# A selective-scan mixer: C's rows spread over the partitions by transfers, two banks for B, and one run of TensorE over the chunks

## The chip, the cores and the metric

The program runs on one core of a Trainium2 chip. The metric is the device time of one execution in microseconds (us); of several runs the median counts. The engines of a core are named TensorE (PE in the profile), VectorE (DVE), ScalarE (ACT), GpSimd (POOL) and SyncE (SP). Each has its own instruction stream in strict order, and they wait for each other by semaphores. A wait stops all that follows it on that engine.

## The reference

The program computes four layers one after the other on x of 2 x 1024 x 128: mixer A, a mixture of experts, mixer B, and the experts again. The change touches mixer A alone. Its reference, cut to what matters:

```
xn = rmsnorm(x)
x_part, z = split(xn @ in_proj_w.T)                  # 256 channels each
u = silu(causal_conv4(x_part) + conv_b)
dt, B, C = split(u @ x_proj_w.T, [8, 24])            # 8, 16 and 16 rows
delta = softplus(dt @ dt_proj_w.T + dt_proj_b)
for t: h = exp(delta_t * A) * h + delta_t * B_t * u_t    # 256 channels x 16 states
       y_t = sum over states of h * C_t
out = ((y + u * D) * silu(z)) @ out_proj_w.T + x
```

## The kernel before, in words

Channels lie on the partitions (two groups f of 128) and time along the rows. The 2048 positions are cut into four chunks g of 512; chunks 0 and 1 are the first sequence, 2 and 3 the second, and `half = g % 2` says whether a state is carried in. In a chunk there are 16 states n, with two steps each, one a channel group: s = 2n + f, 32 steps a chunk.

For one state the work goes over all engines:

- TensorE spreads row n of B over the 128 partitions with a matmul against a selecting matrix (L375, bank B), and row n of C in the same way (L378, bank C). `accumulate(n)` adds hc of both groups to the sums Y by matmuls with the unit matrix (L390); at n = 0 it first puts in u * D (L388, `skip`). An f32 matmul of 128x512 is two records in the trace.
- ScalarE writes the decay exp(delta * A) of a step into one of three banks (L520, three steps ahead of the scan at most), and copies the spread row of C to c_sb (L526), which has two places. In even chunks it saves the last column of h (L511).
- VectorE multiplies delta * u by the row of B for both groups at once (`times_b`, L592) and scans (L607). `times_b(n + 1)` stands between the two scans of state n.
- GpSimd multiplies h by the row of C (L678) into hc, which has four places; so has h.

Beside it the next chunk is prepared, through one PSUM bank O that is used in turn (`in_turn`): two convolutions (TAPS0, TAPS1: eight records each, L319), x_proj (XPROJ, L337), two dt_proj (DT0, DT1, L343), two products for z (Z0, Z1, L325), and for the chunk before, the output projection (PROJECT, L349). Which state each stands behind is written out by hand in the TensorE stream, as are ScalarE's reads of the bank in `between` (steps 3, 5, 12, 17, 19, 25, 27; at 6 the two Silus with their table loads, at 20 and 21 the softplus) and GpSimd's additions and products (steps 21, 23, 25). VectorE multiplies the finished sums of the chunk before by silu(z) after state 1 (`gate`, L574), adds the projection after state 3 (`add`, L579) and makes the low rows after state 6 (`low_rows`, L567: B and C are kept as a rounded high part and a rest, both in `rows`). `accumulate(0)` of a chunk overwrites Y and so waits for the gate.

`half_sequence` of TensorE (L368 to L414) orders a chunk: broadcast(0), TAPS0, broadcast(1), then for n from 2 to 15 broadcast(n), accumulate(n - 2) and the piece of other work that is due, and at the end accumulate(14) and accumulate(15). broadcast(n) waits for times_b(n - 1), since B has one bank.

Before the loop (L416 to L434, L534 to L557, L623 to L653) the norm is made, and chunk 0 is prepared with seven products in banks 0 to 3; ScalarE does the absolute value and the Relu of the softplus (L456, L457) and two copies of z (L555). SyncE issues loads of weights at the start of the stage (L303 to L310) and has nothing to do after them until the next stage.

Of the kernel before, what the change touches and what calls it, by code (L numbers as in the profile page):

```python
# [16 lines left out]
P = 128  # L17
# [56 lines left out]
def cols(c):  # L74
    return slice(c * CH, (c + 1) * CH)
# [169 lines left out]
def mixer_a_stage(k, d):  # L245
# [6 lines left out]
    def sem(name):  # L252
# [4 lines left out]
    DEPTH = 4  # L257
    w_in = sb("w_in", [P, 2 * DI])
# [11 lines left out]
    dt_row = sb("dt_row", [40, T])  # L270
# [3 lines left out]
    c_sb = sb("c_sb", [P, 2, CH])  # L274
    state = sb("state", [P, STEPS])
    yz = sb("yz", [P, FT, CH])
    Y, B, O, C, A = 0, 2, 3, 4, 5
# [3 lines left out]
        o_read, u_ready, rows_high, dt_kept, rows_done, rest_done, exp_done, log_done, delta_ready, du_ready, \  # L281
        z_ready, b_ready, c_ready, c_copied, decay_ready, bu_ready, scanned, saved, hc_ready, y_added, yz_ready, \
        x_folded = [sem(n) for n in (
            "w_loaded taps_loaded pad_zero folded taps_ready skip_ready sel_set a_ready first_ready first_read o_ready "
            "o_read u_ready rows_high dt_kept rows_done rest_done exp_done log_done delta_ready du_ready "
            "z_ready b_ready c_ready c_copied decay_ready bu_ready scanned saved hc_ready y_added yz_ready "
            "x_folded").split()]
# [11 lines left out]
    with stage, nc.Block() as block:  # L299

        @block.sync
        def _(sp):
# [7 lines left out]
            sp.dma_start(k.xn_rows[0:1, :], d["eye"][0:1, :]).then_inc(k.first_row, 16)  # L310

        @block.tensor
        def _(pe):

            def convolution(c, f, bank):
                b, t0 = divmod(c * CH, SEQ)
                for tap in range(TAPS):
                    off = PADC + t0 - (TAPS - 1) + tap
                    last = nc.tensor.matmul(ps[:, bank, :], w_tap[:, f, tap, :], xp[:, b, off:off + CH],  # L319
                                            start=(tap == 0), stop=(tap == TAPS - 1))  # L320
# [20 lines left out]
            def dt_proj(c, f, bank):  # L341
                pe.wait_ge(dt_kept, c + 1)
                return nc.tensor.matmul(ps[:, bank, :], w_dt[32:40, f * P:(f + 1) * P], dt_row[32:40, cols(c)],  # L343
# [8 lines left out]
            def in_turn(g, what):  # L352
# [3 lines left out]
                if what in (TAPS0, TAPS1):  # L356
                    last = convolution(g + 1, what - TAPS0, O)
                elif what == PROJECT:
# [9 lines left out]
            def half_sequence(g):  # L368
                at = cols(g)

                def broadcast(n):
                    m = g * NST + n
                    if m:
                        pe.wait_ge(bu_ready, m)
                    nc.tensor.matmul(ps[:, B, :], sel[:, n, :], rows[:, at], start=True, stop=True).then_inc(b_ready, 1)  # L375
                    if m:
                        pe.wait_ge(c_copied, m)
                    nc.tensor.matmul(ps[:, C, :], sel[:, NST + n, :], rows[:, at], start=True, stop=True)\  # L378
                        .then_inc(c_ready, 1)

                def accumulate(n):
                    for f in range(FT):
                        s = n * FT + f
                        if n == 0:
                            if g:
                                pe.wait_ge(yz_ready, (g - 1) * FT + f + 1)
                            u_done(g)
                            nc.tensor.matmul(ps[:, Y + f, :], skip[:, f, :], u[:, f, at], start=True, stop=False)  # L388
                        pe.wait_ge(hc_ready, g * STEPS + s + 1)
                        nc.tensor.matmul(ps[:, Y + f, :], k.eye[:, :], hc[:, s % DEPTH, :],  # L390
                                         start=False, stop=(n == NST - 1)).then_inc(y_added, 1)

                if g:
                    pe.wait_ge(o_read, use(g - 1, XPROJ) + 1)
                broadcast(0)
                if g + 1 < NCH:
                    in_turn(g, TAPS0)
# [1828 lines left out]
```

## Time and profile before

| | us |
|---|---|
| median of 3 runs | 1179.07 |
| runs | 1178.4 to 1183.63 |
| the profiled execution's own time | 1185.69 |
| its span in the profile | 1183.9 |
| mixer A: loop, first times_b to end of the last scan | 44.90 to 342.3 |
| mean granted TensorE clock of the profiled execution | 0.938 |
| busy over the span: PE, DVE, ACT, POOL | 1032.6, 750.7, 641.3, 575.4 |

The span is shorter than the execution's time by what lies around it. Mixer A's stage ends at about 348.5 us; the rest of the span belongs to the other three layers. In the profile a granted clock of 1.0 is 2.4 GHz and 0.5 is 1.2 GHz; a value between them is a mean over a stretch that has both. PE's busy time is modelled and records overlap a little; PEld are its weight loads. The names with "a_" are mixer A's tiles, "ps" is PSUM.

### The profile page before, as it was taken

To read this page: it belongs to the slowest core of one execution; us is meant where nothing else is said; L and a number is where in the kernel's file an instruction comes from. 1 tells how busy PE (TensorE), PEld (TensorE's weight loads), DVE (VectorE), ACT (ScalarE), POOL (GpSimd) and SP (SyncE) were. 2 spreads that over 40 slices of the span, in tenths; PEclk is the share of its full clock that TensorE was granted. 3 is DMA by queue.
4 is the path that set the end of the run, shared out by engine and by line. 5 is a ranking of instruction groups with operands and counts; after the bars stand their busy time and mean duration, and the time that the engine had idled before them with its cause. 6 is when DMAs were issued, how large, how long until landed. Compare 5 with 4: busy or idle time off the path is not lost. (4 is left out here: it accounts for less than half of the span.)

```text
span 1183.9 us, 16592 instructions
## 1 busy us (share of the span) xinstructions
PE 1032.6 (87%) x4894; PEld 721.0 (61%) x4894; DVE 750.7 (63%) x1163; ACT 641.3 (54%) x1222; POOL 575.4 (49%) x455
## 2 busy tenths in 40 slices
PE   5788787886888789999999887896986899999997
PEld 2222322322227568999999543663664689999996
DVE  4578597677965955555555567764549545555555
ACT  5567464573645344555555386676553345555553
POOL 2268367465650088853671273641000888353732
PEclk9889899887997999999999987997979999999999
DMA  4000000000013022411210300000140214111103
GB/s 132 0 1 0 1 0 0 1 0 1 0 59 113 1 69 70 102 52 52 70 52 15 92 22 1 1 1 0 34 139 0 64 44 126 59 52 54 54 28 112
DMA packets 47906, 49.52 MB, mean 42 GB/s; under 512 B 5000, under 2 KB 39568, under 8 KB 47824
## 3 DMA queue, kind: packets, MB, share of 16 engines
q1 hardware_dynamic: 42832, 38.22, 10.5%
q0 software_dynamic: 4992, 10.23, 3.5%
q8 instruction: 48, 0.79, 0.3%
q14 instruction: 34, 0.28, 0.1%
HBM read 38.08 MB, written 10.36 MB: 41 GB/s over the span
## 5 line engine op out<-in xcount | busy, mean ns | idle before, releaser
L678 POOL TENSOR_TENSOR a_hc<-a_h,a_c_sb 128x512 f32<-128x512 f32 x128 | 160.3, 1268 | 125.5 <-DVE a_h L607 112.0
L390 PE MATMUL ps<-a_hc,eye 128*128 128x512 f32 x256 | 148.0, 684 | 17.2 <-POOL a_hc L678 15.4
L592 DVE TENSOR_TENSOR a_b_u<-a_du,ps 128x1024 f32<-128x1024 f32 x64 | 77.0, 1204 | 58.0 <-PE ps L375 58.0
L390 PEld LDWEIGHTS ps<-a_hc,eye 128*128 128x128 f32 x256 | 44.2, 201 | 91.6 <-POOL a_hc L678 59.9
L520 ACT ACTIVATE ps<-a_delta,a_neg_a 128x512 f32<-128x512 f32 x128 | 86.8, 685 | 20.0 <-DVE a_h L607 19.9
L870 POOL CAST g_ring_rounded<-g_ring 128x1876 fp32r<-128x1876 f32 x8 | 14.1, 1758 | 154.2 <-DVE g_table L1385 104.2
L607 DVE TENSOR_TENSOR_SCAN a_h<-ps,a_state,a_b_u 128x512 f32<-128x512 f32 x64 | 79.1, 1268 | 2.8 <-ACT ps L520 2.5
L607 DVE TENSOR_TENSOR_SCAN a_h<-ps,a_b_u 128x512 f32<-128x512 f32 x64 | 75.3, 1208 | 6.9 <-ACT ps L520 6.7
L526 ACT ACTIVATE a_c_sb<-ps 128x512 f32<-128x512 f32 x64 | 38.0, 593 | 76.6 <-PE ps L378 49.7
L1014 PE MATMUL ps<-g_ring_rounded,g_q_hi_rounded 128*128 x312 | 77.0, 337 | 0.0
L1014 PE MATMUL ps<-f_ring_rounded,f_q_hi_rounded 128*128 x312 | 77.0, 337 | 0.0
L1016 PE MATMUL ps<-f_ring_rounded,f_q_lo_rounded 128*128 x312 | 69.6, 223 | 0.0
L1016 PE MATMUL ps<-g_ring_rounded,g_q_lo_rounded 128*128 x312 | 69.6, 223 | 0.0
L870 POOL CAST f_ring_rounded<-f_ring 128x1876 fp32r<-128x1876 f32 x8 | 14.1, 1760 | 113.4 <-DVE f_table L1385 69.6
L1450 DVE TENSOR_TENSOR g_prods<-g_work,ps 128x470 f32<-128x470 f32 x78 | 49.8, 638 | 28.0 <-PE ps L1042 28.0
L1450 DVE TENSOR_TENSOR f_prods<-f_work,ps 128x470 f32<-128x470 f32 x78 | 49.8, 638 | 27.5 <-PE ps L1042 27.5
L1040 PE MATMUL ps<-f_ring_rounded,f_work_rounded 128*128 x156 | 62.3, 399 | 1.9 <-DVE f_work_rounded L1441 1.5
L1040 PE MATMUL ps<-g_ring_rounded,g_work_rounded 128*128 x156 | 62.4, 400 | 1.7 <-DVE g_work_rounded L1441 1.3
L1155 ACT ACTIVATE g_work<-ps 128x470 f32<-128x470 f32 x78 | 44.0, 563 | 31.3 <-PE ps L1042 31.3
L1155 ACT ACTIVATE f_work<-ps 128x470 f32<-128x470 f32 x78 | 43.9, 563 | 31.2 <-PE ps L1042 31.2
L1014 PEld LDWEIGHTS ps<-g_ring_rounded,g_q_hi_rounded 128*128 128x128 f32 x312 | 58.9, 189 | 2.8
L1014 PEld LDWEIGHTS ps<-f_ring_rounded,f_q_hi_rounded 128*128 128x128 f32 x312 | 58.9, 189 | 2.8
(451 smaller groups left out, 2965.6 us busy)
## 6 DMA issues: line engine op xcount, KB each, us to landing
f_ring<-in_gu SPq DMA_DIRECT2D x16, 469.0 KB, 4.4
g_ring<-in_gu SPq DMA_DIRECT2D x16, 469.0 KB, 4.4
f_ring<-in_dn SPq DMA_DIRECT2D x8, 512.0 KB, 6.1
g_ring<-in_dn SPq DMA_DIRECT2D x8, 512.0 KB, 5.6
xn_rows<-f_work SPq DMA_DIRECT2D x8, 256.0 KB, 2.7
f_rows<-token_rows SPq DMA_DIRECT2D x8, 256.0 KB, 4.8
xn_rows<-g_work SPq DMA_DIRECT2D x8, 256.0 KB, 2.8
g_rows<-token_rows SPq DMA_DIRECT2D x8, 256.0 KB, 4.8
```

What stands on the lines that cost most here:

```text
L390: nc.tensor.matmul(ps[:, Y + f, :], k.eye[:, :], hc[:, s % DEPTH, :], start=False, stop=(n == NST - 1)).then_inc(y_added, 1)
L520: nc.scalar.activation(ps[:, A + m % NA, :], delta[:, f, cols(g)], ACT.Exp, scale=neg_a[:, f, n:n + 1])\
L526: nc.scalar.activation(c_sb[:, n % 2, :], ps[:, C, :], ACT.Copy).then_inc(c_copied, 1)
L592: nc.vector.tensor_tensor(decayed_in[:, p:p + FT, :], du[:, :, cols(g)], ps[:, B, :].unsqueeze(1).to_broadcast([P, FT, CH]), ALU.mult)\
L607: nc.vector.tensor_tensor_scan(h[:, s % DEPTH, :], ps[:, A + m % NA, :], decayed_in[:, s % DEPTH, :], initial, ALU.mult, ALU.add).then_inc ...
L678: nc.gpsimd.tensor_tensor(hc[:, s % DEPTH, :], h[:, s % DEPTH, :], c_sb[:, n % 2, :], ALU.mult)\
L870: nc.gpsimd.tensor_copy(high, raw).then_inc(w_high, 1)
L1014: nc.tensor.matmul(ps[:, Y2, 0:2 * P], q_hi[:, j % 2, a], in_ring(place, w, w + 2 * P), start=(i == 0), stop=False, skip_group_check=True)
L1016: last = nc.tensor.matmul(ps[:, Y2, 0:P], q_lo[:, j % 2, a], in_ring(place, w, w + P), start=False, stop=(i == TILES - 1), skip_group_chec ...
L1040: nc.tensor.matmul(out, xt[:, 0, j % 2, :], w_hi, start=True, stop=False)
L1155: nc.scalar.activation(gates[:, half, 0:HALVES[half]], ps[:, 2 * half, 0:HALVES[half]], ACT.Silu)\
L1450: nc.vector.tensor_tensor(prods[:, j % 2, half * H0:half * H0 + HALVES[half]], gates[:, half, 0:HALVES[half]], ps[:, 2 * half + 1, 0:HALVE ...
```

## The change

Row n of C no longer goes through TensorE, bank C and ScalarE. ScalarE keeps all 40 rows of x_proj's result as they are (x_rows, in place of the 8 rows of dt); SyncE stores C's 16 rows of the chunk in DRAM (c_rows) and then, for each state, issues a transfer that reads one row of 512 values into all 128 partitions of c_sb, which has four places (RING). GpSimd waits for the transfer. The bank that C held goes to B, which alternates between banks 2 and 3; O is bank 4.

TensorE's, VectorE's and ScalarE's streams no longer stop at a chunk's end: broadcast(m) is followed by accumulate(m - 2) for m from 0 to 63, and the first product with B of the next chunk stands between the last two scans. The last three saves of an even chunk come in the first steps of the next. The convolutions are issued in two halves, behind states 0 and 1 (TAPS0) and 2 and 3 (TAPS1); PROJECT, XPROJ, DT0 and DT1 come one state later. ScalarE's reads, the Silus (step 9) and the softplus (steps 21, 22), VectorE's `add` and `low_rows`, and GpSimd's pieces (21, 23, 27) move too. Before the loop VectorE does the two Relus and the two copies of z that ScalarE did.

The diff, cut to its core (runs of removed lines that the listing above shows are left out):

```diff
--- before.py
+++ after.py
@@ -255,6 +255,7 @@
...
     DEPTH = 4
+    RING = 4
     w_in = sb("w_in", [P, 2 * DI])
...
@@ -267,24 +268,26 @@
...
     rows = sb("rows", [64, T], F32R)
-    dt_row = sb("dt_row", [40, T])
+    x_rows = sb("x_rows", [40, T])
+    c_rows = nc.dram_tensor("c_rows", (NST, T), F32, kind="Internal").ap()
     decayed_in = sb("b_u", [P, DEPTH, CH])
...
     hc = sb("hc", [P, DEPTH, CH])
-    c_sb = sb("c_sb", [P, 2, CH])
+    c_sb = sb("c_sb", [P, RING, CH])
     state = sb("state", [P, STEPS])
     yz = sb("yz", [P, FT, CH])
-    Y, B, O, C, A = 0, 2, 3, 4, 5
+    Y, B, O, A = 0, 2, 4, 5
     NA = 3
...
+    c_loaded = [sem(f"c_loaded{i}") for i in range(RING)]
...
@@ -308,13 +311,23 @@
...
             sp.dma_start(k.xn_rows[0:1, :], d["eye"][0:1, :]).then_inc(k.first_row, 16)
+            for g in range(NCH):
+                sp.wait_ge(rows_kept, g + 1)
+                sp.dma_start(c_rows[:, cols(g)], x_rows[NST:2 * NST, cols(g)]).then_inc(rows_stored, 16)
+                sp.wait_ge(rows_stored, (g + 1) * 16)
+                for n in range(NST):
+                    m = g * NST + n
+                    if m >= RING:
+                        sp.wait_ge(hc_ready, (m - RING + 1) * FT)
+                    sp.dma_start(c_sb[:, m % RING, :], c_rows[n:n + 1, cols(g)].partition_broadcast(P))\
+                        .then_inc(c_loaded[m % RING], 16)
 
...
 
-            def convolution(c, f, bank):
+            def convolution(c, f, bank, first=0, end=TAPS):
                 b, t0 = divmod(c * CH, SEQ)
-                for tap in range(TAPS):
+                for tap in range(first, end):
                     off = PADC + t0 - (TAPS - 1) + tap
...
@@ -354,8 +367,9 @@
...
                 if what in (TAPS0, TAPS1):
-                    last = convolution(g + 1, what - TAPS0, O)
-                elif what == PROJECT:
+                    convolution(g + 1, what - TAPS0, O, 0, TAPS // 2)
+                    return
+                if what == PROJECT:
                     last = project(g - 1, O)
...
@@ -365,53 +379,43 @@
...
 
-            def half_sequence(g):
...
+            def between(g, n):
+                if g + 1 < NCH:
+                    if n in (0, 2):
+                        in_turn(g, TAPS0 + n // 2)
+                    if n in (1, 3):
+                        convolution(g + 1, n // 2, O, TAPS // 2, TAPS).then_inc(o_ready, 1)
+                if g and n == 4:
+                    in_turn(g, PROJECT)
+                if g + 1 < NCH:
+                    if n == 6:
+                        in_turn(g, XPROJ)
+                    if n in (8, 9):
+                        in_turn(g, DT0 + n - 8)
+                    if n in (11, 12):
+                        in_turn(g, Z0 + n - 11)
+
+            def broadcast(m):
+                g, n = divmod(m, NST)
+                if n == 0 and g:
                     pe.wait_ge(o_read, use(g - 1, XPROJ) + 1)
-                broadcast(0)
...
+                if m >= 2:
+                    pe.wait_ge(bu_ready, m - 1)
+                nc.tensor.matmul(ps[:, B + m % 2, :], sel[:, n, :], rows[:, cols(g)], start=True, stop=True)\
+                    .then_inc(b_ready, 1)
+
+            def accumulate(m):
+                g, n = divmod(m, NST)
+                for f in range(FT):
+                    s = m * FT + f
+                    if n == 0:
+                        if g:
+                            pe.wait_ge(yz_ready, (g - 1) * FT + f + 1)
+                        u_done(g)
+                        nc.tensor.matmul(ps[:, Y + f, :], skip[:, f, :], u[:, f, cols(g)], start=True, stop=False)
+                    pe.wait_ge(hc_ready, s + 1)
+                    nc.tensor.matmul(ps[:, Y + f, :], k.eye[:, :], hc[:, s % DEPTH, :],
+                                     start=False, stop=(n == NST - 1)).then_inc(y_added, 1)
 
...
@@ -431,9 +435,15 @@
...
             pe.wait_ge(sel_set, 2)
-            pe.wait_ge(first_read, 3 * FT)
-            for g in range(NCH):
-                half_sequence(g)
+            pe.wait_ge(first_read, 2 * FT)
+            pe.wait_ge(z_first, FT)
+            for m in range(NST * NCH):
+                broadcast(m)
+                if m >= 2:
+                    accumulate(m - 2)
+                between(*divmod(m, NST))
+            accumulate(NST * NCH - 2)
+            accumulate(NST * NCH - 1)
             in_turn(NCH, PROJECT)
...
@@ -449,7 +459,7 @@
...
             def keep_rows(c, bank):
-                nc.scalar.activation(dt_row[32:40, cols(c)], ps[32:40, bank, :], ACT.Copy).then_inc(dt_kept, 1)
+                nc.scalar.activation(x_rows[:, cols(c)], ps[0:40, bank, :], ACT.Copy).then_inc(rows_kept, 1)
                 nc.scalar.activation(rows[0:32, cols(c)], ps[0:32, bank, :], ACT.Copy).then_inc(rows_high, 1)
...
@@ -470,32 +480,32 @@
...
                 if c < NCH:
-                    if s in (3, 5):
-                        f = s // 4
+                    if s in (4, 8):
+                        f = s // 8
                         turn(g, TAPS0 + f)
...
                             .then_inc(o_read, 1)
-                if s == 6:
+                if s == 9:
                     if c < NCH:
...
                     else:
-                        act.wait_ge(first_read, 3 * FT)
+                        act.wait_ge(z_first, FT)
                     nc.scalar.activation(both(sz, g), both(sz, g), ACT.Silu).then_inc(z_ready, 1)
...
                 if c < NCH:
-                    if s == 12:
+                    if s == 14:
                         turn(g, XPROJ)
                         keep_rows(c, O)
-                    if s in (17, 19):
-                        f = (s - 17) // 2
+                    if s in (18, 20):
+                        f = (s - 18) // 2
                         turn(g, DT0 + f)
                         parts(c, f, O).then_inc(o_read, 1)
-                    if s == 20:
+                    if s == 21:
                         softplus_exp(c)
-                    if s == 21:
+                    if s == 22:
                         softplus_log(c)
...
@@ -506,8 +516,9 @@
...
 
-                def save(s):
-                    act.wait_ge(scanned, g * STEPS + s + 1)
+                def save(m):
+                    s = m % STEPS
+                    act.wait_ge(scanned, m + 1)
                     nc.scalar.activation(state[:, s:s + 1], h[:, s % DEPTH, CH - 1:CH], ACT.Copy).then_inc(saved, 1)
...
@@ -519,17 +530,9 @@
...
                         .then_inc(decay_ready, 1)
-                    if f == 0:
...
+                    if (half == 0 and s >= NA) or (half == 1 and s < NA):
+                        save(m - NA)
                     between(g, s)
-                if half == 0:
-                    for s in range(STEPS - NA, STEPS):
-                        save(s)
 
...
@@ -546,14 +549,12 @@
...
                 act.wait_ge(first_ready, 4 + f)
-                parts(0, f, bank).then_inc(first_read, 1)
+                nc.scalar.activation(du[:, f, cols(0)], ps[:, bank, :], ACT.Abs, bias=dt_bias(f)).then_inc(rest_done, 1)
             softplus_exp(0)
...
             nc.scalar.preload_act_table_set("exp_and_others")
-            for f, bank in enumerate((1, 2)):
-                act.wait_ge(first_ready, 6 + f)
-                nc.scalar.activation(sz[:, f, cols(0)], ps[:, bank, :], ACT.Copy).then_inc(first_read, 1)
             act.wait_ge(a_ready, 2)
+            act.wait_ge(first_read, 2 * FT)
             act.wait_ge(norm.scaled, NCH)
...
@@ -578,47 +579,40 @@
...
 
-            def half_sequence(g):
+            def times_b(m):
+                g, n = divmod(m, NST)
+                dve.wait_ge(b_ready, m + 1)
+                if n == 0:
+                    dve.wait_ge(du_ready, g + 1)
+                if m * FT >= DEPTH:
+                    dve.wait_ge(scanned, m * FT - DEPTH + FT)
+                p = m % 2 * FT
+                nc.vector.tensor_tensor(decayed_in[:, p:p + FT, :], du[:, :, cols(g)],
+                                        ps[:, B + m % 2, :].unsqueeze(1).to_broadcast([P, FT, CH]), ALU.mult)\
+                    .then_inc(bu_ready, 1)
+
+            def scan(m):
+                g, s = divmod(m, STEPS)
                 half, b = g % 2, g // 2
-
...
+                dve.wait_ge(decay_ready, m + 1)
+                dve.wait_ge(bu_ready, m // FT + 1)
+                if m >= DEPTH:
+                    dve.wait_ge(hc_ready, m - DEPTH + 1)
+                if half == 0 and s >= DEPTH:
+                    dve.wait_ge(saved, b * STEPS + s - DEPTH + 1)
+                if half == 1:
+                    dve.wait_ge(saved, b * STEPS + min(STEPS - DEPTH + s + 1, STEPS))
+                initial = state[:, s:s + 1] if half else 0.0
+                nc.vector.tensor_tensor_scan(h[:, s % DEPTH, :], ps[:, A + m % NA, :], decayed_in[:, s % DEPTH, :],
+                                             initial, ALU.mult, ALU.add).then_inc(scanned, 1)
+
+            def between(g, n):
+                if g and n == 1:
+                    gate(g - 1)
+                if g and n == 4:
+                    add(g - 1)
+                if g + 1 < NCH and n == 7:
+                    low_rows(g + 1, O).then_inc(o_read, 1)
 
...
@@ -644,6 +638,13 @@
...
             low_rows(0, 2).then_inc(rows_done, 1)
+            for f, bank in enumerate((3, 0)):
+                dve.wait_ge(rest_done, f + 1)
+                nc.vector.tensor_scalar(delta[:, f, cols(0)], ps[:, bank, :], k.vec[:, VA_DTB + f:VA_DTB + f + 1], 0.0,
+                                        ALU.add, ALU.max).then_inc(first_read, 1)
+            for f, bank in enumerate((1, 2)):
+                dve.wait_ge(first_ready, 6 + f)
+                nc.vector.tensor_copy(sz[:, f, cols(0)], ps[:, bank, :]).then_inc(z_first, 1)
             dve.wait_ge(log_done, 1)
...
@@ -651,8 +652,13 @@
...
                 .then_inc(du_ready, 1)
-            for g in range(NCH):
-                half_sequence(g)
+            times_b(0)
+            for m in range(NST * NCH):
+                scan(FT * m)
+                if m + 1 < NST * NCH:
+                    times_b(m + 1)
+                scan(FT * m + 1)
+                between(*divmod(m, NST))
             gate(NCH - 1)
...
@@ -671,23 +677,24 @@
...
                     pool.wait_ge(scanned, m + 1)
+                    i = g * NST + n
                     if f == 0:
-                        pool.wait_ge(c_copied, g * NST + n + 1)
+                        pool.wait_ge(c_loaded[i % RING], (i // RING + 1) * 16)
                     if m >= DEPTH:
                         pool.wait_ge(y_added, m - DEPTH + 1)
-                    nc.gpsimd.tensor_tensor(hc[:, s % DEPTH, :], h[:, s % DEPTH, :], c_sb[:, n % 2, :], ALU.mult)\
+                    nc.gpsimd.tensor_tensor(hc[:, s % DEPTH, :], h[:, s % DEPTH, :], c_sb[:, i % RING, :], ALU.mult)\
                         .then_inc(hc_ready, 1)
                     if g + 1 < NCH:
-                        if s == 23:
+                        if s == 21:
                             pool.wait_ge(log_done, g + 2)
...
                                 .then_inc(delta_ready, 1)
-                        if s == 25:
+                        if s == 23:
                             pool.wait_ge(delta_ready, g + 2)
...
                                 .then_inc(du_ready, 1)
-                    if s == 21:
+                    if s == 27:
                         pool.wait_ge(norm.normed, g + 1)
...
```

## Rows read from the trace of the kernel before

**Rows 1.** Windows of the four chunks: length, busy us of each engine (records), clock, DMA.
```profile
44.90:120.47 75.57, 65.93 (x129) 22.51 (x128) 55.58 (x49) 47.04 (x98) 50.44 (x40) 0.90 0.00 1
120.47:198.89 78.42, 64.40 (x133) 22.28 (x132) 59.42 (x52) 43.80 (x66) 50.13 (x39) 0.93 0.00 0
198.89:279.17 80.28, 67.53 (x133) 24.13 (x132) 57.59 (x52) 46.88 (x98) 45.85 (x35) 0.87 0.00 1
279.17:342.30 63.13, 48.16 (x99) 16.09 (x98) 57.90 (x51) 32.75 (x50) 39.77 (x32) 0.92 0.00 0
```

**Rows 2.** Waits of DVE, 44 to 349 us: total us, times, longest.
```profile
DVE a_b_u L592 <- PE ps L375: 58.0, 25, 8.0
DVE a_h L607 <- ACT ps L520: 9.2, 8, 2.2
```

**Rows 3.** Groups of instructions, 44 to 349 us: busy us, mean ns, idle before.
```profile
L678 POOL TENSOR_TENSOR a_hc<-a_h,a_c_sb 128x512 f32<-128x512 f32 x128 | 160.3, 1268 | 125.5 <-DVE a_h L607 112.0 <-PE ps L390 13.3
...
L592 DVE TENSOR_TENSOR a_b_u<-a_du,ps 128x1024 f32<-128x1024 f32 x64 | 77.0, 1204 | 58.0 <-PE ps L375 58.0
L607 DVE TENSOR_TENSOR_SCAN a_h<-ps,a_b_u 128x512 f32<-128x512 f32 x64 | 75.3, 1208 | 6.9 <-ACT ps L520 6.7
...
L526 ACT ACTIVATE a_c_sb<-ps 128x512 f32<-128x512 f32 x64 | 38.0, 593 | 76.6 <-PE ps L378 49.7 <-POOL a_hc L678 26.6
```

**Rows 4.** Timeline of DVE, the late rows of B: start, us, [idle before].
```profile
51.69 1.22 DVE L592 TENSOR_TENSOR a_b_u<-a_du,ps 128x1024 f32<-128x1024 f32 x1 [4.25 <-PE ps L375]
...
61.22 1.22 DVE L592 TENSOR_TENSOR a_b_u<-a_du,ps 128x1024 f32<-128x1024 f32 x1 [2.70 <-PE ps L375]
...
120.47 1.22 DVE L592 TENSOR_TENSOR a_b_u<-a_du,ps 128x1024 f32<-128x1024 f32 x1 [3.70 <-PE ps L375]
...
140.83 1.22 DVE L592 TENSOR_TENSOR a_b_u<-a_du,ps 128x1024 f32<-128x1024 f32 x1 [7.80 <-PE ps L375]
...
203.19 1.22 DVE L592 TENSOR_TENSOR a_b_u<-a_du,ps 128x1024 f32<-128x1024 f32 x1 [1.75 <-PE ps L375]
...
279.17 1.22 DVE L592 TENSOR_TENSOR a_b_u<-a_du,ps 128x1024 f32<-128x1024 f32 x1 [3.92 <-PE ps L375]
...
294.35 1.22 DVE L592 TENSOR_TENSOR a_b_u<-a_du,ps 128x1024 f32<-128x1024 f32 x1 [4.42 <-PE ps L375]
```

**Rows 5.** Timeline before and at the start of the loop, 33 to 46 us.
```profile
33.96 0.59 ACT L452 ACTIVATE a_dt_row<-ps 8x512 f32<-8x512 f32 x1 [0.76 <-PE ps L337]
...
44.10 0.76 PE L375 MATMUL ps<-a_rows,a_sel 64*128 64x512 f32 x1 [3.95 <-ACT a_sz L555]
...
44.90 1.22 DVE L592 TENSOR_TENSOR a_b_u<-a_du,ps 128x1024 f32<-128x1024 f32 x1 [0.83 <-PE ps L375]
```

**Rows 6.** Timeline of PE in chunk 0: TAPS0, rows of B and C, TAPS1.
```profile
45.22 6.01 PE L319 MATMUL ps<-a_xp,a_w_tap 128*128 128x512 f32 x8
51.15 0.50 PE L375 MATMUL ps<-a_rows,a_sel 64*128 64x512 f32 x1
51.49 0.39 PE L378 MATMUL ps<-a_rows,a_sel 64*128 64x512 f32 x1
...
57.16 3.60 PE L319 MATMUL ps<-a_xp,a_w_tap 128*128 128x512 f32 x8
```

**Rows 7.** Timeline at the gate of chunk 1: VectorE's two products, TensorE's skip behind them.
```profile
130.58 1.26 DVE L574 TENSOR_TENSOR a_yz<-ps,a_sz 128x512 f32<-128x512 f32 x2
...
131.30 2.07 PE L388 MATMUL ps<-a_u,a_skip 128*128 128x512 f32 x2 [4.53 <-DVE a_yz L574]
```

**Rows 8.** Timeline of ACT in chunk 0: the Silus' first table load, the decay behind them.
```profile
62.68 1.28 ACT L481 ACT_TABLE_LOAD   x1
...
67.30 0.69 ACT L520 ACTIVATE ps<-a_delta,a_neg_a 128x512 f32<-128x512 f32 x1
```

**Rows 9.** DMA issues by line: count, KB each, median us from issue to landing.
```profile
x<-in_xT SPq DMA_DIRECT2D x4, 256.0 KB, 3.8
...
a_taps<-in_tapsA SPq DMA_DIRECT2D x1, 512.0 KB, 5.8
```

More of the change, by code:

```diff
@@ L273, in mixer_a_stage @@
     hc = sb("hc", [P, DEPTH, CH])
[L274 removed]
+    c_sb = sb("c_sb", [P, RING, CH])
     state = sb("state", [P, STEPS])
     yz = sb("yz", [P, FT, CH])
[L277 removed]
+    Y, B, O, A = 0, 2, 4, 5
     NA = 3
     w_loaded, taps_loaded, pad_zero, folded, taps_ready, skip_ready, sel_set, a_ready, first_ready, first_read, o_ready, \
[L281 to L283 removed]
+        o_read, u_ready, rows_high, rows_kept, rows_done, rest_done, exp_done, log_done, delta_ready, du_ready, \
+        z_ready, b_ready, rows_stored, decay_ready, bu_ready, scanned, saved, hc_ready, y_added, yz_ready, \
+        x_folded, z_first = [sem(n) for n in (
             "w_loaded taps_loaded pad_zero folded taps_ready skip_ready sel_set a_ready first_ready first_read o_ready "
[L285 to L287 removed]
+            "o_read u_ready rows_high rows_kept rows_done rest_done exp_done log_done delta_ready du_ready "
+            "z_ready b_ready rows_stored decay_ready bu_ready scanned saved hc_ready y_added yz_ready "
+            "x_folded z_first").split()]
+    c_loaded = [sem(f"c_loaded{i}") for i in range(RING)]
     norm = Norm(k, "na", sem, sq_at=lambda c: delta[:, 0, cols(c)], joint_at=lambda c: du[:, 0, cols(c)],
@@ L341, in dt_proj @@
             def dt_proj(c, f, bank):
-                pe.wait_ge(dt_kept, c + 1)
-                return nc.tensor.matmul(ps[:, bank, :], w_dt[32:40, f * P:(f + 1) * P], dt_row[32:40, cols(c)],
+                pe.wait_ge(rows_kept, c + 1)
+                return nc.tensor.matmul(ps[:, bank, :], w_dt[32:40, f * P:(f + 1) * P], x_rows[32:40, cols(c)],
                                         start=True, stop=True)
@@ L366, in in_turn @@
                 last.then_inc(o_ready, 1)
-            def half_sequence(g):
[L369 to L393, printed above, removed]
-                    pe.wait_ge(o_read, use(g - 1, XPROJ) + 1)
-                broadcast(0)
-                if g + 1 < NCH:
-                    in_turn(g, TAPS0)
-                broadcast(1)
-                for n in range(2, NST):
-                    broadcast(n)
-                    accumulate(n - 2)
-                    if g + 1 < NCH:
-                        if n == 2:
-                            in_turn(g, TAPS1)
-                        if n == 5:
-                            in_turn(g, XPROJ)
-                        if n in (7, 8):
-                            in_turn(g, DT0 + n - 7)
-                        if n in (11, 12):
-                            in_turn(g, Z0 + n - 11)
-                    if g and n == 3:
-                        in_turn(g, PROJECT)
-                accumulate(NST - 2)
-                accumulate(NST - 1)
@@ L521, in half_sequence @@
                         .then_inc(decay_ready, 1)
-                    if f == 0:
-                        act.wait_ge(c_ready, g * NST + n + 1)
-                        if g or n >= 2:
-                            act.wait_ge(hc_ready, m - 2)
-                        nc.scalar.activation(c_sb[:, n % 2, :], ps[:, C, :], ACT.Copy).then_inc(c_copied, 1)
-                    if half == 0 and s >= NA:
-                        save(s - NA)
+                    if (half == 0 and s >= NA) or (half == 1 and s < NA):
+                        save(m - NA)
                     between(g, s)
-                if half == 0:
-                    for s in range(STEPS - NA, STEPS):
-                        save(s)
             norm.of_scalar(act)
```

38 lines of the change are left out of this document (1 added, 37 removed).

## The prediction

> **What bounds it now.** The windows by chunk come first [rows 1]: mixer A's loop, from its first product with B (44.90 us) to the end of its last scan (342.3 us), takes 297.4 us, and in no chunk is any engine busy throughout. VectorE (DVE) has the most work that can't overlap itself: 49 to 52 records a chunk at 1.13 to 1.14 us each (55.58 / 49, 57.90 / 51), 230.5 us in all. DMA is idle (share 0.00). The waits name what DVE waited for [rows 2]: 58.0 us for a broadcast row of B (L375), 9.2 us for a decay (L520), together 67.2, which is the 297.4 less the 230.5. The groups say what the others do [rows 3]: GpSimd (POOL) is busy 160.3 us with L678, so it is no bound at 2 x 1.27 = 2.5 us a state where DVE needs 1.20 + 2 x 1.21, less 0.1 of overlap each, plus its gates, adds and low rows: 3.5 (55.58 / 16). So DVE's work is a floor, and the time above it is 67 us of waits. Everything after 349 us belongs to the other stages, which the change doesn't touch; I price it at nothing.
>
> The gaps before L592 show where B is late [rows 4]. Three kinds hold most. At the three chunk borders (120.47 the first, 279.17 the last) B(0) comes only after accumulate(14) and (15) of the old chunk: 3.70 + 3.94 + 3.92 = 11.6 us. B(1) stands behind the eight matmuls of TAPS0, three times (51.69 to 203.19): 4.25 + 1.70 + 1.75 = 7.7, and none in chunk 3. B(3) stands behind accumulate(0), which waits for the gate of the chunk before, and behind TAPS1, four times (61.22 to 294.35): 2.70 + 7.80 + 7.99 + 4.42 = 22.9. Of the 58.0 the first B takes 0.8 [rows 5], which leaves 15.0 spread over the rest.
>
> **The change, part by part.** Times of one PE matmul of 128x512 f32 come from the eight of a convolution [rows 6]: 3.60 / 8 = 0.43 us (its last record reaches a little past the next start), against 6.01 / 8 = 0.75 in the first convolution, most of it at the lower level. An accumulate is two of them; B takes 0.34 (51.15 to 51.49).
>
> *PE runs over the borders.* B(16) is issued after accumulate(13), and times_b(16) stands between DVE's scans 30 and 31. The 11.6 go. What would be late next is hc(28), since GpSimd has a fold of 1.27 more at step 27; it makes up 0.5 us a step, and its two double-width additions come two steps earlier than now. I take nothing, at most 0.6 a border.
>
> *TAPS0 in halves.* Four matmuls (1.72) stand before B(1) in place of eight. In the pattern of a state, B + two accumulates + half a convolution = 0.34 + 1.72 + 1.72 = 3.8 us, against DVE's 3.45; PE has about 1.8 us in hand there: the scan that feeds the last hc of accumulate(m-2) ends as scan(2m-2) begins, hc takes 1.27, its accumulate 0.86 and B 0.5, 2.6 us together, and B(m+1) is wanted four DVE operations (4.5 us) after that scan. Four such states cost 4 x 0.35 = 1.4, inside it. In chunk 0 B(0) can start at 41, not 44, so its half at the lower level (3.4 us) ends before scan(0) does. 7.7 becomes 0.6 (0.3 in two chunks).
>
> *The gate.* It stays after scan(3), and accumulate(0) stays behind it [rows 7]. Count from the gate's first start (130.58): 0.7 to yz; skip and accumulate for both halves, 8 x 0.43 = 3.4; half of TAPS1, 1.7; B, 0.5: B(3) at 6.3 us. DVE has its two gate products (1.2) and one scan (1.15) and wants B(3) at 2.3. So 4.0 us stay in chunks 1 and 2 at PE's full clock, and 2.3 in chunk 3, without TAPS1. That is the lower end. The upper end is today's gap less the 1.7 of the half that moves: 6.1, 6.3 and 4.4, because PE was at the lower level in these spots (the chunks' means are 0.87 to 0.93 [rows 1]). PE now idles 4.5 us before the gate; with B over the border (PE done with TAPS0's second half and B(2) about 2 us before the gate's first product is out) it would idle some 3 us. I take nearer the upper end, since the row shows it: 5.6, 5.6, 3.6. In chunk 0 there is no gate: accumulate(0) and half of TAPS1 leave 1.4. 22.9 becomes 16.2 (11.7 to 19.5).
>
> *The rest of PE's 15.0.* Left are: the state after the gate (half of TAPS1, or PROJECT, before the next B), 0.4 in three chunks; DT0 held by DVE's low rows, 0.3 in three; Z1 held until ScalarE (ACT) has read Z0, 0.8 in three; together 4.5. The remainder today is time at the lower level, when a state's matmuls take some 4.1 us (twice 0.34 + 4 x 0.43). The C broadcast leaves (0.3 us a state, 0.6 at the lower level), and with it PE's wait for ACT's copy. I take 4.5 for it, with 0 and 14.5 as ends. 15.0 becomes 9.0.
>
> *The copies of C leave ACT* (64 x 0.59 = 38 us of its time, beside DVE's). The two table loads and two Silus stand between exp(9) and exp(10) now, not exp(6) and exp(7): 4.6 us (62.68 to 67.30 [rows 8]), plus 0.6 + 0.2 before and 0.7 behind, 6.2 after scan(6); DVE has five operations there, 5.6 us, and in chunks 1 and 2 `add` besides. 0.6 once. The softplus has its loads between exp(22) and exp(23): 6 operations of slack against 6 us of ACT; 0.5 in three chunks. 9.2 becomes 2.1 (0 to 5).
>
> *The second bank of B.* B(m+1) is released by times_b(m-1) in place of times_b(m). But in PE's order B(m+1) stands behind accumulate(m-2) all the same, and that ends about when times_b(m) does. I give it 0.2 us of slack a state and nothing of the sum.
>
> *C by transfer.* 64 issues on SyncE (SP), which has nothing else in this stage, at 0.4 us each; in each chunk a store of 32 KB and the wait for it. For one load I have the nearest rows [rows 9]: 256 KB in 3.8 us with four in flight, and a partition broadcast of 512 KB in 5.8. The ring of four is refilled when hc of state m-4 is done, over three states (10 us) ahead. The store (2 to 4 us) falls between the loads of states 15 and 16, which are 3.4 us apart. Cost nothing; if the cover were gone, GpSimd would wait and DVE with it four steps later. Chunk 0: the copy of dt's rows, which takes in C's now, starts at 33.96 [rows 5]; store and first load land by 42 (at 4 us each 43), and the first use is after scan(0), at 45.
>
> *Small moves.* The copy of dt's rows takes 40 partitions for 8 in the same time (the two copies of one x_proj now take 0.59 each, of 8 and of 32 partitions); the last three saves of a carried state go behind the next chunk's first decays, each before its scan asks for it: nothing.
>
> *Before the loop.* ACT loses two Relus and two Copies, DVE gets four such operations while it waits. Exp, Ln and so delta and du come 0.8 to 1.1 earlier, and B(0) no longer waits for ACT's copies [rows 5]: times_b(0) at 43.3 in place of 44.90, 1.6 us. At the end the later fold adds 0.3.
>
> **Sum.** Waits of 11.6 + 7.7 + 22.9 + 15.0 + 9.2 = 66.4 become 0 + 0.6 + 16.2 + 9.0 + 2.1 = 27.9: 38.5 less. With 1.6 at the start and 0.3 lost at the end: 39.8 us. The profiled execution (1185.69) would go to 1145.9. It lies 6.6 above the median of the three runs shown; from that median, 1179.07 - 39.8 = **1139**. Of its own terms this case spans a gain of 23 (19.5 at the gate, 14.5 of clock, 5 at ACT) to 51: 1128 to 1156.
>
> **The rivals.**
> *Only the borders pay* (0.14). DVE, freed, meets the next late B; PE's clock keeps the other gaps at their size. Gain 11.6 + 7.1 + 1.6 = 20.3: 1159. For it: the large gate gap stays behind the same wait. Against: the half of TAPS1 leaves it by the order alone.
>
> *PE at the lower level* (0.03 slower, 0.03 level). The trace first: the means of 0.90, 0.93, 0.87 and 0.92 are 57 us of 297 at 1.2 GHz (twice one less the mean, by each stretch), and falls follow stretches with little work, as before the gate. The change takes 64 matmuls of C out of PE's stream. At 1.2 GHz the 64 states take 64 x 4.1 = 262 us, and the other 112 f32 matmuls of the loop (48 of TAPS, 16 of skip, 12 each of XPROJ, DT, Z and PROJECT) 112 x 0.86 = 96: 358 us, 61 more than now, 1240 on the median's scale. At full clock both take 180. It decides once PE is at 1.2 GHz for 235 of 297 us (235 / 358 + 62 / 180 = 1), four times today's. Against: a PE that is always busy got its clock back each time, as within the first convolution: 6.01 for eight, the next eight 3.60 [rows 6]. The Trainium skill, TensorE: Matmul & The Clock Gate (Part 1), speaks against this change: "the default state is throttled, and activity releases the throttle", so less work in PE's stream is a risk. By the sum above the trace agrees with the rule, but the same rule gives the clock back when PE falls behind, and so it bounds the loss.
>
> *C comes late* (0.03), the case that ends slower. The place is GpSimd's wait for c_loaded; the price is the transfer's throughput. The loop is slower than before once one 256 KB broadcast takes over 297.4 / 64 = 4.65 us of the queue's time, below 56 GB/s. At 6 us each the loop takes 384 us: 1266. For it: 128 reads of one row of 2 KB, of which this trace has none. Against: 512 KB of broadcast landed in 5.8 us with its fixed part, 90 GB/s [rows 9].
>
> *The change does less than it says* (0.05): halves of TAPS and the second bank undo each other in a queue in strict order, and gaps move on behind the border; within 6 us of now.
>
> **Numbers.** Forecast 0.72, borders only 0.14, level 0.08 (0.05 and 0.03), slower 0.06 (0.03 of the clock, 0.03 of C). Half a percent, 6 us, is about what a measurement of this kernel tells from no change. So faster 0.86, same 0.08, slower 0.06. The range takes the forecast's own span, the borders-only case and 3 us for runs that differ by as much: 1125 to 1160.
>
> **What would show it.** In the changed trace: DVE without a gap at the three borders; 4 to 6 us before B(3) in chunks 1 and 2 and 2 to 4.5 in chunk 3; no wait of GpSimd for c_sb; loop length near 258 us and DVE's busy time unchanged at 230; the waits for the decay near 2 us. A wait of GpSimd on a transfer, or PEclk below 0.8 over the loop, would prove me wrong; so would a loop above 280 us.

## The result, and the profile after

The changed kernel takes 1149.08 us (median of 4 runs, 1144.13 to 1151.89), the kernel before 1181.35 in the same comparison: a ratio of 0.9722, 95% interval 0.9676 to 0.9768. The forecast was 1139, the range 1125 to 1160. The profiled execution took 1151.89, its span is 1150.1, 33.8 us shorter than before. The windows of its four chunks and of its whole loop, with the columns of [rows 1] (length, busy us of TensorE, of its weight loads, of VectorE, ScalarE and GpSimd with their records, mean clock, DMA share and GB/s):

```profile
43.84:108.76 64.92, 58.28 (x107) 19.51 (x106) 55.63 (x50) 39.54 (x82) 48.75 (x39) 0.88 0.20 58
108.76:181.01 72.25, 62.43 (x116) 21.52 (x114) 59.28 (x53) 36.48 (x51) 49.38 (x40) 0.88 0.18 59
181.01:248.39 67.38, 57.11 (x116) 19.84 (x116) 57.37 (x53) 39.62 (x81) 45.64 (x36) 0.97 0.21 63
248.39:310.60 62.21, 46.88 (x88) 15.43 (x89) 57.78 (x52) 24.42 (x34) 42.00 (x35) 0.93 0.22 59
43.84:310.60 266.76, 224.70 (x425) 76.30 (x424) 230.07 (x204) 140.05 (x248) 185.77 (x146) 0.92 0.20 60
```

The loop takes 266.8 us for 297.4, VectorE's busy time in it is the same (230.1 for 230.5), ScalarE's is 30 us less, and the mean clock stays (0.92; 0.91 before). So what went is waiting. The waits in the loop, as in [rows 2]:

```profile
ACT ps L531 <- DVE a_h L606: 111.1, 85, 8.9
DVE a_b_u L590 <- PE ps L404: 35.6, 26, 7.2
...
DVE a_h L606 <- ACT ps L531: 0.6, 1, 0.6
```

The wait for a decay is one row of 0.6 us now (9.2 before), and ScalarE, which no longer copies C, waits for VectorE's scans instead. GpSimd has no wait for a transfer; SyncE's own waits in the loop are for GpSimd's products to free a place (240.0 us), so its queue has time to spare. The late rows of B, VectorE's timeline as in [rows 4]:

```profile
54.66 1.22 DVE L590 TENSOR_TENSOR a_b_u<-a_du,ps 128x1024 f32<-128x1024 f32 x1 [1.30 <-PE ps L404]
...
84.41 1.22 DVE L590 TENSOR_TENSOR a_b_u<-a_du,ps 128x1024 f32<-128x1024 f32 x1 [2.96 <-PE ps L404]
...
127.38 1.22 DVE L590 TENSOR_TENSOR a_b_u<-a_du,ps 128x1024 f32<-128x1024 f32 x1 [7.22 <-PE ps L404]
...
197.16 1.22 DVE L590 TENSOR_TENSOR a_b_u<-a_du,ps 128x1024 f32<-128x1024 f32 x1 [4.21 <-PE ps L404]
...
263.32 1.22 DVE L590 TENSOR_TENSOR a_b_u<-a_du,ps 128x1024 f32<-128x1024 f32 x1 [4.38 <-PE ps L404]
```

Sorted as the prediction sorted them (us of VectorE's waiting in the loop, from that timeline; the last column is a second profile of the same kernel, e11_changed_again):

| before what | before | forecast | changed | again |
|---|---|---|---|---|
| B(0) at the borders | 11.6 | 0 | 0 | 0 |
| B behind TAPS0 | 7.7 | 0.6 | 2.1 | 2.1 |
| B(3), behind the gate and TAPS1 | 22.9 | 16.2 | 17.1 | 12.5 |
| B elsewhere | 15.0 | 9.0 | 16.4 | 15.4 |
| a decay | 9.2 | 2.1 | 0.6 | 0.6 |

### The profile page after: what moved, and what is told of

It is laid out like the page before. It is cut to its first block and busy times, and to the rows that moved or that the text cites. A ratio compares the mean times of both kernels' runs of the same rounds, so it can differ in the third digit from the quotient of the medians.

```text
span 1150.1 us, 16414 instructions
## 1 busy us (share of the span) xinstructions
PE 1012.2 (88%) x4830; PEld 713.5 (62%) x4830; DVE 752.6 (65%) x1167; ACT 609.5 (53%) x1154; POOL 575.6 (50%) x455
## 5 line engine op out<-in xcount | busy, mean ns | idle before, releaser
L1023 PEld LDWEIGHTS ps<-g_ring_rounded,g_q_lo_rounded 128*128 128x128 f32 x312 | 59.8, 192 | 0.1
```

What stands on the lines that cost most here:

```text
L1023: last = nc.tensor.matmul(ps[:, Y2, 0:P], q_lo[:, j % 2, a], in_ring(place, w, w + P), start=False, stop=(i == TILES - 1), skip_group_chec ...
```

## The experiments

All ratios are against the kernel before on the same chip; "waits" are VectorE's for B and for a decay in the loop of the profiled run, in us. Where two forms ran on different chips, their difference is given by the ratios.

**One bank for B.**
```diff
-                if m >= 2:
-                    pe.wait_ge(bu_ready, m - 1)
-                nc.tensor.matmul(ps[:, B + m % 2, :], ...
+                if m:
+                    pe.wait_ge(bu_ready, m)
+                nc.tensor.matmul(ps[:, B, :], ...
```


> The changed kernel with one bank for B again: broadcast(m) waits for times_b(m-1), all else as changed. Theory A (the order of TensorE's stream sets when B comes, the second bank hardly matters): within 3 us of the changed kernel's 1149, sum of the waits for B 36 to 39 us. Theory B (the second bank is what lets B come early): the steady states lose 0.2 us or more each, 64 x 0.2 = 13 us, about 1162.

1154.79 us, 0.9761 (0.9726 to 0.9795), waits 36.5 + 0.6. The waits spoke for theory A, the median stood between the two, so both forms ran again side by side:

> The changed kernel once more, to compare it with the one-bank form on the same chip in the same rounds. Both theories: 1144 to 1152 us.

> e1_one_bank once more. Its first median stood 5.7 us above the changed kernel's, its profiled waits for B only 0.9 us above (36.5 for 35.6). Theory A (the second bank is worth 1 us in this order): within 3 us of e11_changed_again. Theory B (it is worth 5 to 6 us): 1154 to 1156.

Changed: 1152.79 us, 0.9741 (0.9708 to 0.9774), a little above what was expected of it. One bank: 1152.05, 0.9736 (0.9705 to 0.9767), waits 33.7 + 0.6. Theory A: in this order the second bank is worth nothing that can be measured (0.9741 and 0.9736, with intervals of 0.003 to each side).

**C by matmul and copy** (on one bank for B; L378's matmul behind each B, L526's copy behind each even step's decay; no store, no transfers).

> As e1_one_bank, and C's rows spread by matmul and copied by ScalarE again, within the stream that runs over the borders; no store, no transfers. Theory A (C's path is worth what it takes off TensorE at the lower clock and off ScalarE's chain at the table loads): 6 to 12 us slower than e1_one_bank, the waits for the decay back to 3 to 8 us. Theory B (C's path is hidden beside VectorE in both): within 3 us of e1_one_bank. Theory C (the transfers cost something that the profile doesn't show as a wait): faster than e1_one_bank.

1167.2 us, 0.9881 (0.9840 to 0.9922), waits 41.2 + 5.8: against the two runs of the one-bank form (0.9761, 0.9736) 1.2 to 1.5%, some 14 to 17 us. Theory A, with the price above its range. One path of it shows in the waits: TensorE waits 9.9 us in three places for ScalarE to read Z0 (up to 3.5 at once; 0.9 in all with one bank and C by transfer), and the rows of B behind them are 2.5 to 3.0 us late.

**TensorE's half of it alone** (on one bank for B, transfers kept).
```diff
+                nc.tensor.matmul(ps[:, 3, :], sel[:, NST + n, :], rows[:, cols(g)], start=True, stop=True)
```


> As e1_one_bank, with C by transfer, but TensorE also spreads C's row into the free bank and nobody reads it: its result is the same, 64 matmuls of 0.34 us more. Theory A (less work lowers TensorE's clock): the mean clock over the loop rises from 0.92 to above 0.94, and the time is the same as e1_one_bank or up to 5 us faster. Theory B (the clock isn't moved by 64 short matmuls; they only stand before the next B): clock within 0.02, waits for B 2 to 6 us more, time up to 6 us slower.

1158.43 us, 0.9813 (0.9768 to 0.9858), waits 39.3 + 0.6, mean clock over the loop 0.92 (0.91 and 0.92 in the one-bank form). Theory B: the mean clock of the loop did not rise with 64 short matmuls more. The matmuls of C cost 0.5 to 0.8% by the point values, but the four times scatter from 1152.71 to 1164.45 and the interval overlaps or touches those of the one-bank form, so this part is weakly shown. What e2 has beyond e3, 0.7% or 8 us, is by subtraction ScalarE's copy with the waits tied to it, of which 5.2 us show as waits for decays.

**Stop at the borders.**
```diff
+                if m and m % NST == 0:
+                    accumulate(m - 2)
+                    accumulate(m - 1)
                 broadcast(m)
-                if m >= 2:
+                if m % NST >= 2:
```
(and the first `times_b` of a chunk behind the last scan.)

> The changed kernel, but TensorE ends a chunk with accumulate(14) and (15) before it spreads the first row of B of the next, and VectorE's first product of a chunk stands behind its last scan. Theory A: the three border gaps come back, 3 x 3.7 to 4.5 = 11 to 14 us, about 1161. Theory B (the wait before B(3) behind the gate takes up what the border loses): part of it is given back there, 4 to 8 us slower only.

1160.15 us, 0.9804 (0.9770 to 0.9837), waits 46.9 + 0.6. The gaps at the three borders are back with 3.20 + 3.09 + 3.20 = 9.5 us, and the 2.1 behind TAPS0 are gone, 7.4 us more in all. The time is 7 to 10 us above the changed kernel's by the ratios (0.9722 and 0.9741). That lies between the two theories: the gaps return as theory A said, a little smaller, and a part is given back as theory B said, but behind TAPS0 and not before B(3) (15.8 us, for 17.1 and 12.5). The waits as a whole stand 11.3 above the changed kernel's, since B elsewhere took 21.6 us in this profile; the profile is that of the slowest of the four executions (1167.78), with a mean clock of 0.89 in the loop for 0.92, and the edit doesn't touch those places.

**Whole convolutions** (TAPS0 behind state 0, TAPS1 behind state 2).

> The changed kernel with each convolution in one piece, TAPS0 behind state 0 and TAPS1 behind state 2. Theory A: before B(3) 1.7 us more in three chunks (5 us), and 1.7 less one state later, where TensorE was 0.5 late, so back 0.5 each; before the second row of B after a border 1 to 1.5 us in two chunks. Together 5 to 7 us slower, about 1155. Theory B (the sum of the gaps depends on TensorE's work alone, not on where it stands): within 2 us.

1157.81 us, 0.9793 (0.9760 to 0.9825), waits 40.6 + 0.8: 5.2 us of waits and 5 to 9 us of time more. Before B(3) stand 21.5 us (17.1 changed), before the rows behind TAPS0 4.5 (2.1). Theory A.

**Each row of C loaded twice.**
```diff
+                    for again in range(2):
+                        if again:
+                            sp.wait_ge(c_loaded[m % RING], (m // RING * 2 + 1) * 16)
                         sp.dma_start(c_sb[:, m % RING, :], ...
```


> The changed kernel with each row of C loaded twice into the same place, the second after the first has landed; GpSimd waits for the second. A transfer lands 3.3 us after its issue. Theory A (C's transfers have slack): the pair takes 6.6 us for one place of four, about the ring's lead of 10 us with the issues in strict order, 2 x 3.3 = 6.6 us a state against 3.5 to 4.1 of the loop, so SyncE's queue becomes the bound and GpSimd waits some 2.5 us a state: 150 us slower. This measures the price of a C that comes late, and shows that no wait is hidden now: every wait of GpSimd for a transfer must turn up as VectorE's wait for hc. Theory B (the loop has lead enough to hide it): within 10 us of the changed kernel.

1202.36 us, 1.0152 (1.0118 to 1.0187): slower than the kernel before, yet neither theory's number: 53 us above the changed kernel, for 150 or at most 10. The loop takes 309.4 us, 4.8 a state, not 6.6, because the second load of a row is not waited for before the next row's first. SyncE's waits, and those of the other engines, in the loop:

```profile
SPq L325 <- DMA a_c_sb<-c_rows: 251.1, 62, 4.8
```
```profile
DVE a_b_u L593 <- PE ps L407: 76.1, 45, 5.9
...
POOL a_hc L688 <- issue: 35.7, 18, 5.1
```

251.1 / 62 = 4.05 us for a landing, and some 2 x 0.43 of issue, make the 4.9 a state: SyncE is never free. A late C does not show as VectorE's wait for hc. GpSimd's wait for a transfer stands as "issue" (only one of them, 2.0 us, is named as a wait for c_sb), and VectorE waits for B, since B stands behind the accumulates that stand behind hc. TensorE's mean clock in the loop is 0.83 here, for 0.92: part of the price may be that, and the two were not parted. The single load has its cover: in the changed kernel GpSimd has no such row, and the row of its DMA issues reads

```profile
a_c_sb<-c_rows SPq DMA_DIRECT2D x64, 256.0 KB, 3.3
```

**B a state ahead.** The order of TensorE's stream made the gaps, so the order should remove them:
```diff
                 broadcast(m)
-                if m >= 2:
-                    accumulate(m - 2)
+                if m >= 3:
+                    accumulate(m - 3)
                 between(*divmod(m, NST))
+            accumulate(NST * NCH - 3)
```


> The changed kernel with broadcast(m) followed by accumulate(m-3) in place of accumulate(m-2), so B(3) and the first half of TAPS1 stand ahead of the wait for the gate; the second bank makes this possible. Theory A (what stands before B in TensorE's order is the whole of the remaining waits): the gaps before B(3) (1.3 + 7.2 + 4.2 + 4.4 = 17 us) become a small gap before B(4), 1 us each, and gaps at the lower clock shrink by half: the waits for B 36 to 10 or 15 us, time about 1126 to 1130. Theory B (with B early, GpSimd's hc, which waits for the accumulates behind the gate, is late next): a new wait of VectorE's scans for hc of 2 to 3 us at each gate, and a gain of only 8 to 12 us.

1132.6 us, 0.9586 (0.9561 to 0.9610), waits 17.2 + 0.6, loop 246.9. The gate of chunk 1 in its timelines, VectorE and then TensorE:

```profile
117.27 1.19 DVE L591 TENSOR_TENSOR a_b_u<-a_du,ps 128x1024 f32<-128x1024 f32 x1
...
121.50 1.22 DVE L591 TENSOR_TENSOR a_b_u<-a_du,ps 128x1024 f32<-128x1024 f32 x1 [0.67 <-PE ps L404]
```
```profile
112.88 1.99 PE L332 MATMUL ps<-a_xp,a_w_tap 128*128 128x512 f32 x4 [0.16 <-ACT a_u L487]
114.80 0.50 PE L404 MATMUL ps<-a_rows,a_sel 64*128 64x512 f32 x1
115.62 1.12 PE L415 MATMUL ps<-a_u,a_skip 128*128 128x512 f32 x2 [0.32 <-DVE a_yz L576]
```

Half of TAPS1 and B(3) are issued before TensorE asks for the gate, which it then waits 0.32 us for, and the 7.22 us before VectorE's product with B(3) (117.27 here) are gone, with 0.67 before the next. In chunk 0, which has no gate, 1.05 us stay before B(3) and 2.31 stand before B(4). Theory A, except that the gain (16 to 20 us) falls a few us short of it; no wait of a scan for hc appears (theory B).

> As e6_b_ahead (B a state ahead of the accumulates), but with one bank for B. Theory A (the second bank pays only where the order uses it: with B ahead, one bank makes TensorE wait for times_b(m-1) before every B, so the accumulates and the next pieces stand behind that wait): 5 to 15 us slower than e6_b_ahead's 1132.6, waits for B above 22 us. Theory B (the order alone does it, the bank nothing): within 3 us of e6_b_ahead.

1136.42 us, 0.9595 (0.9552 to 0.9638), waits 23.2 + 0.6. The waits are theory A's, 6 us more; the times are theory B's: 0.9586 and 0.9595 can't be told apart. Whether the second bank pays in this order stays open; that the order does most of it alone is plain.

**The pieces moved.** DT0 and DT1 one state later, Z0 and Z1 behind states 12 and 14 (ScalarE's read at 29); once on B ahead, once on the changed kernel.

> As e6_b_ahead, with DT0 and DT1 one state later and Z0 and Z1 behind states 12 and 14 (ScalarE reads Z1 at step 29). Theory A (those matmuls hold B because they wait for VectorE's low rows and for ScalarE's read): the gaps of 0.3 to 0.8 us at those places go, 2 to 5 us faster than e6_b_ahead. Theory B (with B ahead they are hidden already): within 2 us of it.

> The changed kernel (accumulate(m-2) as changed) with DT0 and DT1 one state later and Z0 and Z1 behind states 12 and 14, nothing else. Theory A (TensorE standing idle for VectorE's low rows, and for ScalarE's read of Z0, is what lets its clock fall in each chunk's second half, and the gaps of 2 to 3 us there are that): the gaps there (13.8 us outside border, gate and the state behind it) fall to 4 to 7 us, time 7 to 10 us below the changed kernel. Theory B (the clock falls whatever stands where, since too little work is in the stream): the gaps move to other states with the same sum, within 3 us of the changed kernel.

On B ahead: 1123.45 us, 0.9499 (0.9454 to 0.9545), waits 8.3 + 3.9, loop 241.0. It is the fastest of all, 5% below the kernel before. On the changed kernel: 1150.14, 0.9731 (0.9693 to 0.9768), no gain. VectorE's waits of the latter in the loop:

```profile
DVE a_b_u L590 <- PE ps L404: 25.4, 17, 5.8
DVE a_h L606 <- ACT ps L531: 7.5, 7, 2.2
```

The waits for B fell as theory A said (from state 6 of each chunk on, from 13.7 to 6.0), but the time did not fall by its 7 to 10 us: dt_proj one state later made ScalarE's softplus late, and with it the decays behind: 7.5 for 0.6 us. With B ahead TensorE reaches dt_proj earlier and only 3.9 come back.

## Why the prediction was right, and where it was off

*VectorE's work is the floor and the rest is waiting:* shown. Its busy time stayed at 228.4 to 232.2 in every form of the loop, and the loop followed the waits from 241.0 us (12.2 of waits) over 266.8 (36.2) to 297.4 (67.2).

*The borders, 11.6:* right. They vanished, and e4 brought back 9.5 of them, less the 2.1 that it took away behind TAPS0. *The halves of the convolutions:* right in kind; e5 gives 5.2 us of waits, at the gate and behind TAPS0 together. B behind TAPS0 kept 2.1, not 0.6: the two states that follow a border each end 0.2 to 0.8 late.

*The gate, 16.2 within 11.7 to 19.5:* right, 17.1 and 12.5 in two profiles. At full clock chunk 2 shows 4.21 where 4.0 was worked out; at the lower level chunk 1 showed 7.22, over my upper end of 6.1, because the gap before the change, from which I took it, had its clock back sooner: 4 us behind the gate there, 6 here (mean 0.50 from 118 to 124 us). TensorE's idle time before the gate was 3.0 to 4.7 us for the 3 forecast. Which level it comes out at is not told by the length of the standstill alone. These are its first matmuls behind the gates of chunks 1 and 2:

```profile
118.43 2.08 PE L415 MATMUL ps<-a_u,a_skip 128*128 128x512 f32 x2 [3.09 <-DVE a_yz L575]
...
191.29 1.12 PE L415 MATMUL ps<-a_u,a_skip 128*128 128x512 f32 x2 [3.03 <-DVE a_yz L575]
```

After 3.09 us the two take 2.08 us, after 3.03 only 1.12, at a clock of 1.00 (188 to 198 us). e6, which changes the order alone, takes the gaps before B(3) out of chunks 1 to 3.

*B elsewhere, 9.0:* this is the step that failed; it measured 16.4 and 15.4, no less than before. I had 0.3 us a chunk for DT0 held by VectorE's low rows, and 4.5 in all for time at the lower clock. At this one place the two meet. TensorE's timeline in the changed kernel:

```profile
75.98 1.24 PE L356 MATMUL ps<-a_x_rows,a_w_dt 8*128 8x512 f32 x2 [1.60 <-DVE a_rows L568]
77.15 0.79 PE L404 MATMUL ps<-a_rows,a_sel 64*128 64x512 f32 x1
...
83.58 0.79 PE L404 MATMUL ps<-a_rows,a_sel 64*128 64x512 f32 x1
```

It stands 1.60 us for the low rows, its clock falls (mean 0.57 from 76 to 88 us), and the state with DT1 in it takes 6.4 us (77.15 to 83.58): the gap of 2.96 at 84.41. Chunks 1 and 2 have 2.13 and 1.31 at the same place, after waits of 1.72 and 1.60 us for the low rows; with the gaps one state earlier they make 8.2 us of the 16.4 (6.1 of the 15.4 in the second profile). With the pieces one state later (e7, e9) these gaps are gone from that place, and smaller ones stand behind it, before B(11) and B(12): 0.93 + 0.41 us in chunk 0 of e7, 1.51 + 0.43 in chunk 1 of e9.

Why the clock falls there stays open. The order of events speaks for the standstill: in each chunk the clock falls within 2.5 us of DT0's wait, to 0.50 from 77 to 87, 152 to 162 and 221 to 223 us. Other rows speak against it as the whole cause. After a wait of 1.99 us at 173.58, and the 3.03 at 191.29, the clock stayed at 1.00. In e9 DT0 has no wait for the low rows any more, and in chunks 0 and 2 the clock stays up there, but in chunk 1 it is 0.50 from 149.5 to 159 us after waits of no more than 0.91. And in e7 TensorE still stands 1.60 us for the low rows in chunk 0 and is at 0.50 from 78.5 to 91.5 us; what VectorE then waits for B is 1.3 us, since B is a state ahead. So the sure part is that the lower clock and the wait together held B at this place; what part each has, no run parts, and the clock was not changed by itself.

*ScalarE, 2.1:* it was 0.6, the single 0.6 that was worked out. *Transfers, nothing:* right, 3.3 us a landing. *The second bank, nothing:* right. *The start, 1.6:* 1.1 (43.84 for 44.90), but in the other runs, which have the same code ahead of the loop (all but e2), the first product stands anywhere from 42.78 to 45.89, so the term can't be told from that spread. *The end, 0.3:* 0.8; GpSimd's fold at step 27 leaves its last four products back to back. The other three layers took 2.9 us less in this execution than in the one before, with nothing changed in them; such spreads are as large as several terms of the sum.

So of a forecast gain of 39.8 us 32.3 came by the medians (29.6 in the second comparison). The waits that were to stay at 27.9 us stayed at 36.2: 7.4 more for B elsewhere, 1.5 behind TAPS0, 0.9 at the gate, and 1.5 less for decays. In the second profile they are 30.6: the same term is 6.4 too large there, and the gate, 3.7 under its forecast, hides it. How far the sum as a whole is off so differs from execution to execution, 8.3 or 2.7 us of waits, and part of its nearness in the second is luck; that B elsewhere was put too low holds in both.

*Only the borders pay* is out: against the 7 to 10 us of e4 stand 14 to 17 for C's path (e2) and 5 to 9 for the halves (e5). *TensorE at the lower level* is out: the clock's mean did not fall (0.92 and 0.94 for 0.91 before), and C's matmuls did not raise it (0.92 in e3, 0.91 and 0.92 in the one-bank form). The rule of the Trainium skill (TensorE: Matmul & The Clock Gate, Part 1), that activity releases the throttle, is not contradicted by it, only the fear that I drew from it: 64 matmuls of 0.34 us made no difference to the clock that shows. *C comes late* is out for the single load, and e8 shows its price, since the point from which it decides lies near: 4.8 us a state made the kernel slower than before (1.0152), as the 4.65 of the prediction had it.

## What to carry to other kernels

In a queue in strict order ask of each short matmul that feeds the bounding engine what stands ahead of it, and put it ahead of whatever waits: issuing each row of B one accumulate earlier gained another 1.4 to 1.6%, half as much as the whole change or more, and the second bank alone gained nothing. A piece that waits for another engine can cost more than its wait, since TensorE often, though not always, came out of it at the lower clock here; read that from the lengths of the matmuls behind it. Moving a piece later to spare one engine moves the wait to the engine behind it, so count the waits of all of them.

## What the runs showed that was not expected

- A wait of GpSimd for a transfer is mostly a wait on "issue" in the profile, and what VectorE then shows is a wait for TensorE (e8: 35.7 and 76.1 us).
- The same kernel's loop took 266.8 and 260.8 us in two profiles, with a mean clock of 0.92 and 0.94 and gate gaps of 7.22 and 4.15 us in chunk 1: which level TensorE is at when it meets a wait differs from run to run. The spread of 0.7% in the four times goes with it (the fastest, 1144.13, has a mean clock of 0.950 over the whole execution, the slowest, 1151.89, 0.942).
- One row of 2 KB read by 128 partitions (256 KB written) lands in 3.3 us, no later than 256 KB of x with four in flight (3.8 [rows 9]); with each row loaded twice the median is 4.1.
